# A graph network on one core: the channel norm of the edge slots goes over turned rows, as the dense rows' does

## What is computed

```python
h = fused @ fus_w + fus_b
mean = jnp.mean(h, axis=0)
var = jnp.mean((h - mean) ** 2, axis=0)
h = (h - mean) * jax.lax.rsqrt(var + BN_EPS) * bn_gamma + bn_beta
return jax.nn.relu(h)
...
x = _layernorm(x + _L2_gnn_ref(x, edge_index, ...), axis=-1)
```

## Time and profile before

| | |
|---|---|
| median of 3 runs | 14892.31 us (14879.5 to 14901.67) |
| the profiled execution, its own time | 14902.41 us |
| its span, first to last instruction | 14900.7 us |
| busy in the span | PE 34%, VectorE (DVE) 57%, ScalarE (ACT) 25%, GpSimd (POOL) 57% |
| mean granted clock of TensorE | 0.614 of full speed |
| stage `cheb_norm`, first DMA issue to the next stage's first | 12070.7 to 12748.7 us, 678.0 us |

### The profile page before, as it was taken

The page is one execution under the profiler, slowest core; times in us unless marked ns, Lnnn a source line. Parts: engine busy times, 40 slices in busy tenths (PEclk is TensorE's granted clock), DMA queues, the critical chain, the costliest instruction groups (busy, mean ns, idle before and its releaser), DMA issues. The chain is left out here.

```text
span 14900.7 us, 104766 instructions
## 1 busy us (share of the span) xinstructions
PE 5032.5 (34%) x25061; PEld 4094.7 (27%) x25061; DVE 8526.5 (57%) x13835; ACT 3799.2 (25%) x9597; POOL 8529.7 (57%) x8672
## 2 busy tenths in 40 slices
PE   0000012000000002100015335576409976888876
PEld 0000002000000001100014334455308866666544
DVE  8860345444444445422577679776644468558765
ACT  0000011000000001100442342466402357654431
POOL 0567777777777777777227630477673410540767
PEclk9855555555555555555555555677659976899555
DMA  6200234433433344311565433344324457777753
GB/s 212 110 5 1 60 96 133 117 111 111 118 111 110 111 119 123 108 54 54 176 210 160 116 102 127 112 136 129 109 78 131 134 200 272 245 243 246 219 166 107
DMA packets 953813, 1967.82 MB, mean 132 GB/s; under 512 B 322912, under 2 KB 330957, under 8 KB 949616
## 3 DMA queue, kind: packets, MB, share of 16 engines
q1 hardware_dynamic: 674928, 1585.65, 31.2%
q0 software_dynamic: 278272, 375.46, 11.2%
HBM read 1192.75 MB, written 783.59 MB: 133 GB/s over the span
## 5 line engine op out<-in xcount | busy, mean ns | idle before, releaser
L724 POOL DMA_INDIRECT hop_odd_raw<-hop_table,i_hop x1176 | 1112.3, 946 | 393.6 <-issue 371.3
L724 POOL DMA_INDIRECT hop_even_raw<-hop_table,i_hop x1176 | 1112.3, 946 | 387.9 <-issue 348.5
L520 POOL DMA_INDIRECT gine_raw<-x,dst_other x392 | 380.4, 970 | 815.1 <-POOLq L89 695.9
L520 POOL DMA_INDIRECT cheb_raw<-x,i_near x392 | 445.7, 1137 | 654.3 <-POOLq L89 535.1
L520 POOL DMA_INDIRECT gine_raw<-conv,i_near x392 | 396.4, 1011 | 611.7 <-POOLq L89 492.4
L1773 POOL DMA_INDIRECT own_raw<-x,i_dst x392 | 388.0, 990 | 602.9 <-POOLq L89 483.7
L981 POOL DMA_INDIRECT mid<-cheb_slots_ends_rows,dst_end x392 | 384.0, 980 | 490.0 <-DVEq L1488 372.9
L1563 PE MATMUL cheb_slots_ends_product<-folded,b_slots_ends_turned_rows 97*128 97x292 f32 (+3 forms) x3136 | 659.6, 353 | 0.0
L1563 PE MATMUL cheb_base_product<-folded,cheb_base_turned_rows 97*128 97x292 f32 x1568 | 565.4, 517 | 180.4 <-ACT cheb_base_mixed L1517 180.4
L748 DVE TENSOR_TENSOR hop_even_rows<-hop_even_raw,hop_even_factors 128x672 f32<-128x672 f32 x168 | 144.9, 862 | 750.1 <-DMA hop_even_raw<-hop_table,i_hop 750.1
L748 DVE TENSOR_TENSOR hop_odd_rows<-hop_odd_raw,hop_odd_factors 128x672 f32<-128x672 f32 x168 | 144.9, 862 | 750.1 <-DMA hop_odd_raw<-hop_table,i_hop 750.1
(11 more groups left out here) (556 smaller groups left out, 22542.2 us busy)
## 6 DMA issues: line engine op xcount, KB each, us to landing
hop_odd_res<-hop_table SPq DMA_DIRECT2D x168, 336.0 KB
hop_table<-hop_odd_sums SPq DMA_DIRECT2D x168, 336.0 KB
hop_even_res<-hop_table SPq DMA_DIRECT2D x168, 336.0 KB
hop_table<-hop_even_sums SPq DMA_DIRECT2D x168, 336.0 KB
start_x_x<-x_and_map SPq DMA_DIRECT2D x98, 400.0 KB, 3.8
x<-start_x_rows SPq DMA_DIRECT2D x98, 400.0 KB
cheb_base_term<-x SPq DMA_DIRECT2D x98, 400.0 KB
mid<-cheb_base_rows SPq DMA_DIRECT2D x98, 400.0 KB
```

The costliest lines, as they stand in the source:

```text
L520: pool.indirect_dma_start(out=raw_rows[:, b % RAW, g, :], out_offset=None, in_=table, in_offset=bass.IndirectOffsetOnAxis(ap=index[:, t:t ...
L724: pool.indirect_dma_start(out=raw_rows[:, b % RAW, g, :], out_offset=None, in_=table, in_offset=bass.IndirectOffsetOnAxis(ap=index[:, t:t ...
```

## The change

The slot job becomes a `ChannelNormRows` too, with `scaled_by_act` false, so that its last scaling stays with VectorE. Class `NormRows` goes, and with it the spread coefficients: their tile, the two diagonals, the matmul and the copy in `batch_norm`.

```diff
-class NormRows(Rows):
...
-            nc.vector.tensor_tensor(mid, mid, self.wide(0), ALU.mult).then_inc(self.sem(ph, "scaled"), 1)
-            dve.wait_ge(self.sem(ph, "scaled"), i + 1)
-            nc.vector.tensor_tensor(mid, mid, self.wide(1), ALU.add).then_inc(self.sem(ph, "moved"), 1)
...
-            nc.vector.scalar_tensor_tensor(rows, mid, 0.0, self.tiles["x"][:, m, :, 0:C], ALU.max, ALU.add)\
-              .then_inc(self.sem(ph, "filled"), 1)
-        self.vector_norm(ph, dve, q)
...
@@ batch_norm
-    with Phase(nc, "batch", ["loaded", "own", "rooted", "varied", "ready", "wide"]) as ph:
+    with Phase(nc, "batch", ["loaded", "own", "rooted", "varied"]) as ph:
...
-        wide = ph.psum("wide_rows", [P, 512])
...
-            own.step(nc.vector.tensor_scalar(diagonal[:, 0, :], k.ident[0:C, 0:C], square, None, ALU.mult))
-            own.step(nc.vector.tensor_scalar(diagonal[:, 1, :], k.ident[0:C, 0:C], shift, None, ALU.mult))
-            own.wait()
-            dve.sem_inc(s["ready"], 1)
-            dve.wait_ge(s["wide"], 1)
-            own.step(nc.vector.tensor_copy(k.coefficients[:, :, :].rearrange("p a c -> p (a c)"), wide[:, 0:2 * C]))
...
-            pe.wait_ge(s["ready"], 1)
-            nc.tensor.matmul(wide[:, 0:2 * C], k.ones[0:C, :], diagonal[:, :, :].rearrange("c a n -> c (a n)"),
-                             start=True, stop=True).then_inc(s["wide"], 1)
...
-        self.coefficients = sb("coefficients", [P, 2, C])
...
@@ graph_layers
     slot_rows(nc, k, "cheb_norm", ChannelNormRows(nc, k, "x3", True, (0, batches), x2, mid, x3, True),
-                  (NormRows(nc, k, "ends", False, slots, x2_slots, mid_slots, x3_slots),))
+                  (ChannelNormRows(nc, k, "ends", False, slots, x2_slots, mid_slots, x3_slots, False),))
```

More of the change, by code:

```diff
@@ L1620, in scalar @@
         self.scalar_norm(ph, act, q)
-class NormRows(Rows):
[L1627 to L1651, removed]
-            nc.vector.tensor_tensor(mid, mid, self.wide(0), ALU.mult).then_inc(self.sem(ph, "scaled"), 1)
-            dve.wait_ge(self.sem(ph, "scaled"), i + 1)
-            nc.vector.tensor_tensor(mid, mid, self.wide(1), ALU.add).then_inc(self.sem(ph, "moved"), 1)
-            if i >= self.DEPTH:
-                self.left(ph, dve, i - self.DEPTH)
-            dve.wait_ge(self.sem(ph, "moved"), i + 1)
-            nc.vector.scalar_tensor_tensor(rows, mid, 0.0, self.tiles["x"][:, m, :, 0:C], ALU.max, ALU.add)\
-              .then_inc(self.sem(ph, "filled"), 1)
-        self.vector_norm(ph, dve, q)
[L1662 to L1666, removed]
 class ChannelNormRows(Linear):
@@ L2482, in _ @@
             nc.scalar.activation(root, square, ACT.Sqrt).then_inc(s["rooted"], 1)
-        @block.tensor
-        def _(pe):
-            pe.wait_ge(s["ready"], 1)
-            nc.tensor.matmul(wide[:, 0:2 * C], k.ones[0:C, :], diagonal[:, :, :].rearrange("c a n -> c (a n)"),
-                             start=True, stop=True).then_inc(s["wide"], 1)
 class Resident:
```

## The result

The changed kernel takes **14816.74 us** (median of 5 runs, 14814.18 to 14821.77) against 14892.31 us: a ratio of 0.9951, 95% interval 0.9937 to 0.9966. The profiled execution took 14814.18 us, its span is 14812.4 us. The forecast was 14857, the range 14800 to 14910: the time lies in the range, near its fast end, and the gain of 75.6 us is over twice the 35 that were forecast.

The account below looks back on a forecast made before the run. A wait, caused by VectorE's 5.9 us slot step, was taken as the bound. 294 pairs x 2.15 us + 12.7 gave a 645 us stage, 33 us saved, with batch_norm's 1.9 some 35: 14857 us, range 14800 to 14910.

Parts of the forecast that it names:

- the wait of 166 us: ScalarE's wait for the slots' centred rows from VectorE, once in each of 49 slot batches; forecast to fall to near nothing.
- One of the prediction's own signs of being wrong: The forecast called itself wrong if TensorE's idle time after the change is put down to loads.
- The product bank is not emptied: Claim that during VectorE's 5.9 us slot step the dense job's add stands behind it, leaving TensorE nothing to do.
- forecast 559: ScalarE's busy time in the stage: 483.7 us plus 98 copies of turned rows at 766 ns, 75.1 us.
- TensorE's share at the low level: Share s of 294 turn-and-product pairs at TensorE's slow clock, 2.51 us each against 1.31; forecast s = 1/3.
- the fill and drain: TensorE's time outside its work at the stage's start and end, 22.3 us; 12.7 us counted, with ScalarE idle.
- 0.07 us for each of 294 pairs: ScalarE's waits for products, taken from 13.9 us over 196 copies before the change, added to 1.90 us a pair.
- s = 0.55: Low-level share deciding the slow-clock rival; the forecast gave s = 0.56, for a stage as long as now less 1.9 us.
- the transfers' case: Rival: waits for loads replace the old wait; if TensorE's 25.8 us double, stage 671 us, kernel 14883; chance 0.20.
- the level did not stay low: Denies the rival that TensorE's clock stays mostly low and bounds a slower kernel, 14939 to 14972 us; chance 0.12.
- a level that stays high: Rival: TensorE's clock stays high, s = 0, stage 592 us, kernel 14804 us; chance 0.20.
- the third: Rival that transfers fill the place of the wait, the same as the transfers' case; chance 0.20.

Follow-up runs that it names:

- e_spread: Kernel before the change, with the slot job's centring moved from VectorE's even to its odd step; stage 621.7 us, ratio 0.9960.
- e_before_lead3: Kernel before the change, with the stage's loads issued three batches ahead (`LEAD = 3`) and nothing else; stage 677.0 us, ratio 0.9997.
- e_lead3: Changed kernel with each load of the stage issued three batches ahead instead of two; stage 576.1 us, ratio 0.9932.
- e_dense_dve: Changed kernel with the dense job's scaling on VectorE in one operation instead of eight on ScalarE; stage 528.0 us, 14740.91 us, ratio 0.9890.

## Why the prediction was right, and where it was not

The time lies in the range, and the mechanism was the forecast one: the wait of 166 us went, ScalarE became the busiest, VectorE and `batch_norm` came out as summed. The size was not: the stage saved 61.9 us where the sum had 33, and 12 us more lie outside the stage and have no shown cause. One of the prediction's own signs of being wrong came true as well, TensorE's idle time is put down to loads.

*The bound before* was named rightly in the main: `e_spread` and `e_before_lead3` show that it was VectorE's even step for the slots, not VectorE's total work, nor the loads; the clock was no better in `e_spread` (0.59) and the stage 56 us shorter. "The product bank is not emptied" is not borne out, since TensorE has no wait for VectorE's adds there; the way went over ScalarE, which stood for the centred rows.

*VectorE*: forecast 347, measured 356 us. *batch_norm*: forecast 1.9 (the rows give 1.96), measured 1.6 us. Both small.

*ScalarE*: forecast 559, measured 548 us. I added 98 copies at their duration of 766 ns. The next operation starts 0.66 us behind the start of such a copy when nothing holds it (a copy of 0.78 us at 12302.06 and a root at 12302.72 in the timeline after), so it begins before the copy has ended, and ScalarE's busy time rose by 64.5 us, 0.66 for each. This is 11 us of the forecast's excess of 29.

*TensorE's share at the low level*: forecast a third of the pairs, in stretches of two to four after some eight at the high level. Counted in the timeline it is 0.27 of the product groups (79) or 0.28 with the 3 mixed ones. (TensorE's busy time, 496.4 less 385 us at 1.20 us more a pair, gives 0.32; that is too much, since busy time also has the tail of the last product ahead of each idle time.) That this came near is in part luck, for the reason was another. I had put it down to ScalarE's eight scalings that hold the copies back, and forecast idle times under 3 us; the slow stretches came behind waits for loads of up to 4.7 us. The forecast's reason is seen in `e_lead3`, where the loads are in time: TensorE's waits for ScalarE's copies, of 1.6 to 1.7 us, precede 14 slow stretches, and the clock is 0.87. The Trainium skill ("TensorE: Matmul & The Clock Gate", section "A second HAM failure mode: psum-queue depth-cycling") has a TensorE that idles briefly between groups swing between its levels and lose throughput. `e_lead3` agrees, with 47 of 294 product groups slow; in the changed kernel the level swung as well, but behind waits for loads.

*The terms that were mis-sized* are the waits for products. The sum had 73 us for them beside ScalarE's work and the fill and drain: 0.07 us for each of 294 pairs, 21 us, and 0.54 us for each of 98 slow pairs, 53 us. Measured are 616.1 - 548.2 - 12.7 = 55 us, of which 43.5 are waits for products. 42.5 us of these stand behind the 79 slow product groups, 0.54 us each as forecast, and 1.0 us behind all those at the high level. So the 0.07 us, 21 us in all, were counted twice: the 13.9 us of the kernel before, from which they came, all stand behind slow products. The slow pairs were fewer than 98, another 10 us. Against both stand 12 us of other waits that the sum lacks, 6.9 of them for the slots' sum of squares.

Two slips in the sums change little: the stage is as long as now *plus* 1.9 us at s = 0.55, not 0.56, and the transfers' case reaches 14910 if its waits grow by 25.8 us once more, not if they double once more.

*The Trainium skill's rule that relu, add and multiply go to VectorE* ("ScalarE: Activation LUTs", section "Rules for kernel authors") did not decide: the moved work cost ScalarE 64.5 us and took 170 off VectorE, and the stage became shorter. `e_dense_dve` agrees with the rule, though, where it is about the other half of the work: one scaling of 958 ns on VectorE in the place of eight on ScalarE (2.2 us) took the stage from 616 to 528 us. The change moved a part of the work that ScalarE does in fewer passes, and the kernel still has a part there that it does in more.

*The rivals*: the level did not stay low, and the stage of 616 us lies between the forecast's 645 and the 592 of a level that stays high. Late loads filled the place of the wait in part (83 us of TensorE's idle time), as the third had it, and cost the stage up to 40 us (`e_lead3`), but ScalarE worked on through most of it, and the stage stayed well under that rival's 671.

## What to carry to other kernels

Look for the step in which one in-order engine waits for a result that another makes late in a long run: another order of the same work can win most of what moving the work wins (56 of 62 us here). Price a moved operation by the distance from its start to the start of what follows it at once, not by its duration. Before adding a wait as it is measured now to a new sum, see behind what it stands; here it stood behind slow pairs, which had a term of their own. And once such a wait is gone, look at which queue issues the loads behind stores that wait: one more batch of lead was worth 40 us where ScalarE had the pace, and the stage was 23 us longer with it where the DMA share was 0.92.

## What was not expected of the hardware

Redundant work on TensorE went with a shorter stage, twice: 1176 transposes more took 22.6 us off at a lead of two and 8.8 us at a lead of three, with the mean granted clock going from 0.80 to 0.96 and from 0.87 to 0.97. At a DMA share of 0.92 the same rise from 0.85 to 0.98 gave nothing (528.0 and 535.3 us), with TensorE itself busy 96% of the stage.
